# Ranking lanes read from a PSUM bank, and part rows loaded in five buffers of two batches

## The reference

```python
m0 = segment_sum(relu(x[src] + edge_attr), dst)                      # layer 0, plus (1 + eps) * x
x1 = segment_sum(w[:, None] * x[dst], src); x2 = the same on x1      # layer 1, w from the degrees
h = relu(segment_sum(x[src], dst) @ w_rel1 + x @ w_root1 + b1)       # layer 2, and once more on h
m3 = relu(segment_sum(edge_weight[:, None] * (x @ w)[src], dst) + b) # layer 3
```

## Time and profile before

| | |
|---|---|
| median of 3 runs | 9735.9 us (9727.46 to 9779.13) |
| profiled execution, its own time | 9638.26 us |
| its span | 9636.5 us |
| DVE busy | 7111.9 us (74%) |
| PE busy | 6840.5 us (71%) |
| POOL busy | 5750.1 us (60%) |
| ACT busy | 4647.4 us (48%) |
| DMA | 2162.48 MB, mean 224 GB/s |

### The profile page before, as it was taken

How to read it: one execution, slowest core, us unless ns; L and a number is a source line. 1 busy time by engine, 2 the same in 40 slices (tenths; PEclk the granted TensorE clock), 3 DMA queues, 4 the chain that set the end, 5 groups by cost and what they waited for, 6 DMA issues and landing times. The chain is left out here.

```text
span 9636.5 us, 224105 instructions
## 1 busy us (share of the span) xinstructions
PE 6840.5 (71%) x65909; PEld 5511.2 (57%) x65909; DVE 7111.9 (74%) x11423; ACT 4647.4 (48%) x13851; POOL 5750.1 (60%) x6132
## 2 busy tenths in 40 slices
PE   9877776767772177799566866685678766867777
PEld 8755554545551166799445744573457545766666
DVE  6655565555554577799877977797779677979997
ACT  0345454544442266644676067506740675069920
POOL 0387787777784066533465556564555465648874
PEclk9855555555555555555666966796679667955588
DMA  9465666654235799744577977896789578936686
GB/s 340 102 176 166 163 175 175 172 157 114 73 75 176 253 306 302 230 122 122 182 270 280 355 243 269 290 350 212 266 293 339 189 270 284 357 132 231 230 305 233
DMA packets 1139377, 2162.48 MB, mean 224 GB/s; under 512 B 391662, under 2 KB 607726, under 8 KB 1138510
## 3 DMA queue, kind: packets, MB, share of 16 engines
q1 hardware_dynamic: 812062, 1231.35, 42.6%
q0 software_dynamic: 224928, 663.45, 18.1%
q10 hardware_dynamic: 101904, 261.43, 8.1%
HBM read 1227.26 MB, written 928.49 MB: 224 GB/s over the span
## 5 line engine op out<-in xcount | busy, mean ns | idle before, releaser
L522 POOL DMA_INDIRECT messages_in_parts<-WORK,goal x1850 | 1999.8, 1081 | 1194.2 <-ACT WORK L690 675.3
L491 POOL DMA_INDIRECT edge_rows<-WORK x1664 | 2101.5, 1263 | 907.9 <-issue 490.6
L923 PE MATMUL psum<-BIG,WORK 128*128 x11840 | 1586.7, 303 | 887.3 <-ACT WORK L690 480.6
L1219 DVE TENSOR_TENSOR WORK<-WORK,psum 128x1024 bf16<-128x1024 uint8 x1480 | 1707.8, 1215 | 621.0 <-remote 511.7
L690 ACT CAST WORK<-psum 128x432 bf16<-128x432 f32 (+1 forms) x4440 | 1765.4, 547 | 602.2 <-remote 390.6
L923 PEld LDWEIGHTS psum<-BIG,WORK 128*128 128x128 bf16 x11840 | 1129.0, 130 | 1344.5 <-issue 942.3
L541 POOL TENSOR_TENSOR BIG<-BIG,WORK 128x48 f32 x2220 | 1214.0, 547 | 972.9 <-ACT WORK L706 393.0
L1016 DVE TENSOR_TENSOR WORK<-lane_k,slot_part 128x1024 bf16<-128x1024 bf16 x2220 | 1548.3, 729 | 24.0 <-remote 13.1
L951 PE MATMUL psum<-WORK 128*128 128x144 bf16 x14800 | 1260.0, 235 | 332.6 <-DVE WORK L1016 273.2
L951 PEld LDWEIGHTS psum<-WORK 128*128 128x128 bf16 x14800 | 1099.7, 147 | 493.4 <-issue 385.4
L929 PE MATMUL psum<-BIG,WORK 128*128 x17760 | 984.3, 214 | 419.6 <-issue 248.1
(11 more groups left out here) (180 smaller groups left out, 10191.7 us busy)
## 6 DMA issues: line engine op xcount, KB each, us to landing
WORK<-messages_in_parts SPq DMA_DIRECT2D x1850, 288.0 KB, 4.5
WORK<-parts_by_slot SPq DMA_DIRECT2D x444, 640.0 KB
BIG<-edge_rows SPq DMA_DIRECT2D x148, 1040.0 KB
messages_in_parts<-BIG ACTq DMA_DIRECT2D x37, 2880.0 KB
WORK<-blocks_by_edge SPq DMA_DIRECT2D x416, 256.0 KB
edge_rows<-BIG ACTq DMA_DIRECT2D x1, 76960.0 KB, 242.8
BIG<-whole_messages SPq DMA_DIRECT2D x370, 193.5 KB, 2.4
whole_messages<-BIG ACTq DMA_DIRECT2D x37, 1920.0 KB
```

The costliest lines, as they stand in the source:

```text
L491: pool.indirect_dma_start(rows_dram, bass.IndirectOffsetOnAxis(ap=at_stage[g][:, j:j + 1], axis=0), row_buf[g][:, j, :], None).then_inc(s_ ...
L522: pool.indirect_dma_start(unit_dram, bass.IndirectOffsetOnAxis(ap=goal[1 - d][:, t:t + 1], axis=0), msg[c].rearrange("p k f -> p (k f)"), ...
L923: m = pe.matmul(o, select[c % GB][:, k, :], V3[:, ds(b * W3, W3)], start=True, stop=True)
L1219: m = v.tensor_tensor(SEL[c % GB], part_row[c // GB][:, c % GB, :], here_p.to_broadcast([128, T * K]), ALU.is_equal)
```

## The change

Two edits that don't touch each other. **Lanes:** `lane_r` goes; the same numbers are copied once, before the ranking, into PSUM bank 6 as float32, and the two compares of a group read them there. **Part rows:** `PR = 2`; there are five buffers of two batches for them in place of two of five (the same bytes in SBUF), with a semaphore each. A load carries two batches (256 KB). SP waits for two selectors, loads two batches, and so on, five times in a turn; the loads of the edges' feature rows keep their two buffers and stand behind the third and the fifth of these. At a pass's start all five part loads are issued, and in the edge pass the two loads of feature rows after them.

```diff
+PR = 2
-        lane_r = sb("lane_r", [128, NBX * RC], U8)
-        lane_rk = lane_r[:, :].rearrange("p (m c) -> p m c", c=RC)
-        part_row = [carve(128, [GB, T * K], U8) for _ in range(2)]
+        part_row = [carve(128, [PR, T * K], U8) for _ in range(RING // PR)]
+        lane_p = bank[6][:, 0:NBX * RC].rearrange("p (m c) -> p m c", c=RC)
-                def load_parts(i, s):
-                    sp.dma_start(part_row[s].rearrange("p a b -> p (a b)"),
-                                 part_dram[1 - d][ds(i * RING + s * GB, GB), :].rearrange("t n -> (t n)")
-                                 .unsqueeze(0).to_broadcast([P, GB * T * K])).then_inc(s_prow[s], 16)
+                def load_parts(i, j):
+                    sp.dma_start(part_row[j].rearrange("p a b -> p (a b)"),
+                                 part_dram[1 - d][ds(i * RING + j * PR, PR), :].rearrange("t n -> (t n)")
+                                 .unsqueeze(0).to_broadcast([P, PR * T * K])).then_inc(s_prow[j], 16)
                 def load_more(i):
-                    for s in range(2):
-                        sp.wait_ge(s_sel, i * RING + (s + 1) * GB + q * BATCHES)
+                    for j in range(RING // PR):
+                        sp.wait_ge(s_sel, i * RING + (j + 1) * PR + q * BATCHES)
                         sp.sem_inc(s_sp_turn, 1)
-                        load_parts(i + 1, s)
+                        load_parts(i + 1, j)
                         if kind == "edge":
-                            sp.wait_ge(s_z, i * RING + (s + 1) * GB)
-                            sp.sem_inc(s_sp_turn, 1)
-                            load_rows(i + 1, s)
+                            for s in range(2):
+                                if j * PR < (s + 1) * GB <= (j + 1) * PR:
+                                    sp.wait_ge(s_z, i * RING + (s + 1) * GB)
+                                    sp.sem_inc(s_sp_turn, 1)
+                                    load_rows(i + 1, s)
-                for s in range(2):
-                    load_parts(0, s)
-                    if kind == "edge":
+                for j in range(RING // PR):
+                    load_parts(0, j)
+                if kind == "edge":
+                    for s in range(2):
                         load_rows(0, s)
-                    m = equal(oh[k][g % RS], lane_rk, blk[k][:, ds(n * RC, RC)])
+                    m = equal(oh[k][g % RS], lane_p, blk[k][:, ds(n * RC, RC)])
-            step(v.tensor_copy(lane_rk, lane_ck[:, :, 0:RC]))
+            step(v.tensor_copy(lane_p, lane_ck[:, :, 0:RC]))
-                    if c % GB == 0:
-                        dve.wait_ge(s_prow[c // GB], i * 16 + (q * PAIRS + 1) * 16)
+                    if c % PR == 0:
+                        dve.wait_ge(s_prow[c // PR], i * 16 + (q * PAIRS + 1) * 16)
```

More of the change, by code:

```diff
@@ L268, in gnn_program @@
         s_value = sem("node_values_ready")
-        s_prow = [sem(f"part_rows_loaded{s}") for s in range(2)]
+        s_prow = [sem(f"part_rows_loaded{s}") for s in range(RING // PR)]
         s_sel, s_spread = sem("selectors_ready"), sem("messages_selected")
@@ L1218, in selector @@
                     if kind == "plain":
-                        m = v.tensor_tensor(SEL[c % GB], part_row[c // GB][:, c % GB, :], here_p.to_broadcast([128, T * K]), ALU.is_equal)
+                        m = v.tensor_tensor(SEL[c % GB], part_row[c // PR][:, c % PR, :], here_p.to_broadcast([128, T * K]), ALU.is_equal)
                     else:
-                        m = v.tensor_scalar(SEL[c % GB], part_row[c // GB][:, c % GB, :], here[:, 0:1], None, ALU.is_equal)
+                        m = v.tensor_scalar(SEL[c % GB], part_row[c // PR][:, c % PR, :], here[:, 0:1], None, ALU.is_equal)
                     m.then_inc(s_sel, 1)
```

## The result

The changed kernel takes 10049.16 us (median of 4 runs, 10028.24 to 10059.6), the kernel before 9731.68 us beside it (4 runs, 9707.01 to 9779.13). The ratio is 1.0318 with a 95% interval of 1.0274 to 1.0361: slower. The forecast was 9379.

What follows compares the result with a forecast made beforehand. The prediction took POOL's scatter issue to bound the ranking. Terms of -501, +70 and +74 us gave 357 us less there, part rows 0, so 9379 us from 9735.9; range 9190 to 9520 us.

Steps and rivals of the forecast that it cites:

- The first term: Ranking: lanes in PSUM end the long scatters, POOL's group falls from 6.27 to 5.07 us, -501 us.
- the second term: Ranking: POOL runs dry longer at each of about ten chain stalls, +7 us x 10 = +70 us.
- the third term: Ranking: block loads arrive late now and then, 2 us for each of 37 turns with fills, +74 us.
- another cause: Rival, ranking: long DMAs only coincide with the compares, so nothing moves, 9736 us; chance 0.04.
- the dear compare: Rival, ranking: compares reading PSUM take three times as long, 1.69 us, +329 us, 10065 us; chance 0.03.
- The part rows: Select halves: smaller, earlier part loads change nothing, value 0, since loads were hardly ever late.
- The plain select halves, forecast at 580 us: Sign, plain passes: a plain select half keeps its 580 us and line 1219 some 500 us of "remote".
- the forecast's bound of +73 us: Edge pass: the most that smaller part loads could cost through extra DMA engine time; 0 was taken.
- The reading of the pauses: Plain passes: DVE's pauses come from the ring DVE, PE, ACT with five selectors, not from part loads; value 0.
- the chain's own speed: Ranking: DVE, PE and ACT take 4.91 us a group unhindered, just under POOL's 5.07, so POOL stays the bound.
- the slower rivals: Outcomes slower than before; the only one listed was the compare from PSUM being dear, 10065 us, chance 0.03.

Runs made afterwards that it cites:

- e6: The kernel before, unchanged, run again in a session without late signals: 9064.96 us, ratio 1.0019 to its own runs beside it.
- e5: The changed kernel, both edits, run again against the kernel before in a session without late signals: 8553.24 us, ratio 0.9458.
- e1: The lanes edit alone against the kernel before, in a session without late signals: 8549.56 us, ratio 0.9428.
- e2: The part rows edit alone, lanes in SBUF, against the kernel before, in a session without late signals: 9061.67 us, ratio 1.0001.
- e12: The lanes edit alone, measured a third time, against the kernel before in a session with late signals: 10027.01 us, ratio 1.0308.
- e7: The lanes edit alone, repeated against the kernel before in a session with late signals: 9914.70 us, ratio 1.0322.
- e13: The lanes edit alone with only two of each group's four scatters issued, against the kernel before, with late signals in the session: 8999.78 us, ratio 0.9337.
- e8: The lanes edit alone plus a POOL memset of 1.28 us before each group of scatters, against the kernel before, session with late signals: 9567.13 us, ratio 0.9935.
- e10: The lanes edit alone plus a POOL memset of 0.69 us per group, against the kernel before, session with late signals: 10072.90 us, ratio 1.0324.
- e11: The lanes edit alone plus a POOL memset of 0.40 us per group, against the kernel before, session with late signals: 10033.42 us, ratio 1.0305.
- e14: The lanes edit alone with features loaded only for eight groups, against the kernel before, session with late signals: 9888.42 us, ratio 1.0259.
- e15: The lanes edit alone plus two more DVE copies from PSUM per group, against the kernel before, session with late signals: 9926.57 us, ratio 1.0298.
- e9: The changed kernel with the plain passes' selectors made by tensor_scalar, no PSUM operand, against the kernel before, session with late signals: 9849.86 us, ratio 1.0255.

## Why the prediction was wrong

**What held.** That the long scatters are those beside the two compares with both inputs in SBUF, 413 of 413, and that the edit takes them away: mean 957 ns for 965 forecast, the longest 1166 ns for below 1200, the compare 560 ns for 560 to 565. The first term, -501 us, is 511 between e6 and e5. That POOL is the bound with the chain under it: 416 x 5.07 = 2108 us, and e1 and e5 have 2100. In such a session the second and the third term are nothing. So the rivals of another cause (0.04) and of the dear compare (0.03) fell. The second had 10065 us as its time, 16 us from the measured one; that is chance, since its mechanism, a compare of 1.69 us, is not there.

The Trainium skill (SBUF — State Buffer, section "Who interferes with whom") has the inference that tensor_tensor leaves descriptor writing alone. For these indirect DMAs the runs show otherwise: line 491 takes 1265 ns in e6 and line 494 takes 958 in e5, with the compares' lanes in SBUF and in PSUM. Whether it is the writing of descriptors that waits or another access of the same instruction, no run tells.

**The part rows** are worth nothing, as I took them (e2: 1.0001), where they were measured apart, without late signals; with them there is only the comparison across sessions, 1.0318 with the part rows for 1.0322 and 1.0308 without. The reason that I gave was in part wrong: part rows can be late (154.7 us in e6), and POOL's rate hides it. "Remote" before line 1222 stayed, 531.0 us for 511.7, as forecast. The plain select halves, forecast at 580 us, are at 614 to 617 between first and last scatter in the profile after, and at first I put this down to the smaller loads. But e12, with the old loads, has 607 to 613 us, and e7, also with the old ones, 584 to 589. It is a difference between executions and sessions, and the profile of before was its fastest execution. The edge half (677 us) goes the same way: 676 in e12, 671 in e7. No run comes near the forecast's bound of +73 us; the largest difference is 612 us in e5 for 600 in e6.

The reading of the pauses, "So the gap belongs to the ring DVE to PE to ACT and back with its five selectors", was wrong. The same ring with the same five selectors takes 467 to 471 us a half in e6 and has no "remote" before line 1219: the pauses are late signals too.

**The step that failed** is the chain's own speed, "4.91 us each", together with the second term, "+7 us x 10 = +70 us": the ranking was to take 357 us less and took 298 more. In the session of the forecast DVE waits 1275 us before the place update and POOL 1241.5 for the slot numbers; the ranking takes 2950 us and not 2295. The 4.91 us were read from one free turn, the price of stalls from a stretch in which POOL was the bound, and both were carried over as constants. They are not. Where no signal is late, 4.91 us was a fair reading (4.77 in e13); in the changed kernel a group takes 7.09 us. The stalls before "remote" are PE's signals coming late. In the kernel before, the long scatters held POOL at 6.27 us a group and it stayed in a state where this happened 27 times in 2550 us. Once the scatters follow each other without the long ones, it happens in nearly every second group, and each costs some 5 us: 174 waits, 963.4 us. The third term plays no part there: DVE's waits for block loads fell from 375.2 to 3.5 us.

What the runs show of the cause: it comes with the lanes alone (e7, e12); goes with a POOL break of 1.28 us per group (e8) and with two scatters in place of four (e13); it stays with breaks of 0.69 and 0.40 us (e10, e11), without SyncE's feature loads (e14), and with a slower DVE (e15); reads from PSUM alone don't make it, since e8 has them all. What they don't show: by which path POOL's scatters delay PE's signals, why some sessions have none of it, and where between 0.69 and 1.28 us the limit lies. Nor is there a run of the ranking with close scatters and no lanes in PSUM, so the two together remain a rival; against it stands e9, whose plain passes have late signals without such reads. I had put no chance on such a case; its place was among the slower rivals, as a chain that is itself slowed by what the faster POOL does.

I could have seen it. The earlier trace rows all hold idle time before "remote" on instructions that wait for PE, I gave the word no owner, and I priced it as if it did not depend on POOL.

Three slips in the numbers changed nothing. A POOL group at 6.27 us makes a turn of 50.2 us, and 8 x 6.37 is the ranking's mean turn, waits included. With the third term at three times its size the forecast is 9527 us, not 9500. Five short scatters touch a one-hot, by 2 to 21 ns, not three.

## What to carry to other kernels

Idle time before "remote" on an instruction whose only producer has long ended is a signal that came late; find out what goes on beside it before taking its price over to a kernel in which that goes faster. When an edit takes the brake off one engine, ask what the others do in the stretches where that engine already ran without its brake, and take many such stretches, not one. And measure a change in more than one session: here the same two kernels stand at 0.946 in one and at 1.032 in another.

## What was unexpected of the hardware

- The same kernel took 9056 us in some sessions and 9620 to 9741 in others, each steady within 1%. Between the profiles of before in the first session and in e6 it is 552 us: 470 in the four plain select halves (2346 for 1877), 60 in the edge one (660 for 600) and 41 in the ranking (2652 for 2610), less 16 behind the last scatter, where e6 is the longer one. The weight select, whose scatters are the longest (median 1560 ns), takes 690 us in both.
- SyncE is slowed in the same stretches: between 400 and 2400 us, 463 of its 2443 recorded instructions take over 0.6 us in the changed kernel, most of them 0.7 us; in e5 it is 70 of 3462. It is no measure of the late signals: e10, with the most "remote", has 169.
- A DMA that POOL is issuing is lengthened by a pair of two-input SBUF compares even when it began before them; so it was in 344 of the 413 long ones.
